# Regrouping the eight-wide heads of a decoder kernel: one 32-row score product per unit, one values block per step

## What is computed

```python
Q, K, V = split(x @ Wq), split(y @ Wk), split(y @ Wv)   # 16 heads of 8
scores = einsum('bhqd,bhkd->bhqk', Q, K) / sqrt(8)
attn = softmax(scores, axis=-1)
out = einsum('bhqk,bhkd->bhqd', attn, V).reshape(B, S, 128) @ Wo
```

## Time and profile before

| | us |
|---|---|
| median of 3 runs | 2144.5 (2141.21 to 2146.36) |
| span of the profiled execution | 2139.6 |
| PE busy in it | 1891.7 (88%) |
| DVE busy | 1520.1 (71%) |
| ACT busy | 1370.0 (64%) |
| POOL busy | 827.2 (39%) |

### The profile page before, as it was taken

How to read it: one execution, slowest core, us unless ns; L and a number is a source line. 1 busy time by engine, 2 the same in 40 slices (tenths; PEclk the granted TensorE clock), 3 DMA queues, 4 the chain that set the end, 5 groups by cost and what they waited for, 6 DMA issues and landing times. The chain is left out here.

```text
span 2139.6 us, 40133 instructions
## 1 busy us (share of the span) xinstructions
PE 1891.7 (88%) x13875; PEld 1361.0 (64%) x13945; DVE 1520.1 (71%) x4153; ACT 1370.0 (64%) x5428; POOL 827.2 (39%) x951
## 2 busy tenths in 40 slices
PE   6998989889998998998888999615899996899998
PEld 5757944535786965874444688404467775467776
DVE  4676788788655666779789855695876664786665
ACT  3686589827654587668963765343677774567666
POOL 2461056615432354025643533111543333543334
PEclk9999999979999999999998999867999998999999
DMA  5000000000001000000000000300000000000000
GB/s 228 1 1 1 2 1 1 1 1 2 1 2 34 1 2 1 1 2 1 1 1 1 1 2 1 111 0 13 1 2 1 1 1 24 1 1 1 1 1 11
DMA packets 6980, 24.79 MB, mean 12 GB/s; under 512 B 752, under 2 KB 3440, under 8 KB 6128
## 3 DMA queue, kind: packets, MB, share of 16 engines
q1 hardware_dynamic: 6768, 22.09, 2.8%
HBM read 21.04 MB, written 1.05 MB: 10 GB/s over the span
## 5 line engine op out<-in xcount | busy, mean ns | idle before, releaser
L1358 POOL TENSOR_TENSOR a_probs<-a_probs,a_rinv 128x512 f32<-128x512 f32 x352 | 367.3, 1044 | 421.9 <-DVE a_rinv L1191 417.5
L997 ACT ACTIVATE a_probs<-score_bank,a_negmax 128x128 f32<-128x128 f32 x896 | 315.7, 370 | 64.5 <-DVE a_negmax L1171 62.8
L1358 POOL TENSOR_TENSOR c_probs<-c_probs,c_rinv 128x512 f32<-128x512 f32 x192 | 201.1, 1047 | 296.2 <-DVE c_rinv L1191 294.2
L836 PEld LDWEIGHTS second_bank<-const,a_probs 128*128 128x128 f32 x1408 | 167.4, 142 | 193.4 <-DVE a_probs_t L1198 101.4
L803 PE MATMUL score_bank<-a_km,a_qg 128*128 128x512 f32 x512 | 267.6, 604 | 2.6 <-issue 0.9
L836 PE MATMUL second_bank<-const,a_probs 128*128 128x128 f32 x1408 | 218.4, 278 | 40.8 <-DVE a_probs_t L1198 32.8
L1366 POOL TENSOR_TENSOR a_rstd<-a_ve,neg_half 128x1 f32<-128x1 f32 x128 | 70.5, 551 | 357.6 <-DVE a_ve L1249 356.2
L1171 DVE TENSOR_REDUCE a_negmax<-score_bank 128x4 f32<-128x512 f32 x224 | 154.0, 687 | 67.7 <-PE score_bank L803 53.0
L997 ACT ACTIVATION_READ_ACCUMULATOR a_probs<-score_bank,a_negmax 128x1 f32 x896 | 188.2, 210 | 0.0
L1198 DVE COPY a_probs_t<-second_bank 128x512 f32<-128x512 f32 x272 | 179.6, 660 | 3.9 <-PE second_bank L836 3.9
L1021 ACT ACTIVATE c_probs_t<-second_bank 128x512 f32<-128x512 f32 x160 | 95.3, 595 | 109.9 <-PE second_bank L836 109.5
(11 more groups left out here) (308 smaller groups left out, 4590.3 us busy)
## 6 DMA issues: line engine op xcount, KB each, us to landing
w_L_ffn<-in_L_ffn SPq DMA_DIRECT2D x1, 3184.0 KB, 14.4
w_L_xattn<-in_L_xattn SPq DMA_DIRECT2D x1, 2112.0 KB, 24.2
w_L_xattn<-in_L_xattn SPq DMA_DIRECT2D x1, 2050.0 KB, 10.3
a_xt<-in_xT SPq DMA_DIRECT2D x3, 512.0 KB, 3.6
a_x<-in_x SPq DMA_DIRECT2D x3, 512.0 KB, 3.7
a_ct<-in_ctxT SPq DMA_DIRECT2D x3, 512.0 KB, 5.8
w_L_attn<-in_L_attn SPq DMA_DIRECT2D x1, 1345.5 KB, 17.2
w_L_attn<-in_L_attn SPq DMA_DIRECT2D x1, 1157.0 KB, 5.8
```

Of the source, the lines that this page charges most:

```text
L836: mm = pe.transpose(bank[:, j * S:(j + 1) * S], Pb[:, n % 4, j * S:(j + 1) * S], ident)
L997: op = act.activation(p, score_bank[n % 3][:, j * width:(j + 1) * width], ACT.Exp, bias=negmax[:, n % 4, j:j + 1], accum_out=rsum[:, n % 4 ...
L1358: pool.tensor_tensor(p, p, along(rinv[:, n % 4, 0:heads], 512 // heads), ALU.mult).then_inc(sems["norm_done"], 1)
```

## The change

Units are now cut the other way. Unit i takes the four heads 4i to 4i+3, which lie in rows 32i to 32i+31. Its score product uses these 32 rows alone: the queries' rows as they are, times `Kz`, the four copies of the keys that POOL spreads and scales by the eight rows of each e (it did that with the queries). The product still has 512 columns, and it is still one per unit and slot. `Km`, its four 32-row writes and `Qg` are gone: ACT writes the keys with one instruction, and the rotation on DVE is one instruction of 128x256 in place of five.

A value product for 32 partitions wants all of its heads' rows at once, so the values are now issued once per step, after i3, as 16 products, and `PT` keeps five units' transposes in place of two. `values` of i0, i1 and i2 issue nothing. The table of relative positions is read with a stride. `Q8` shares its storage with `K64` and `V64`, which are not live together.

```diff
+PT_RING = 5
...
+        if stage == "values":
+
+            return sum(self.kind(s) in SOFTMAX and (self.kind(s) not in H8 or i == 3) for s, i in self.units[:n + 1])
...
-            PT = sb(tag + "probs_t", [P, 2, 512], scope=scope)
+            PT = sb(tag + "probs_t", [P, PT_RING, 512], scope=scope)
...
-            Qg = sb(tag + "qg", [P, 2, 4, S], scope=scope)
-            Km = sb(tag + "km", [P, 2, 4, S], scope=scope)
+            Kz = sb(tag + "kz", [P, 2, 4, S], scope=scope)
...
-                            mm = pe.matmul(bank[:, :], Qg[:, plan.ring(s, 2), i, :], Km[:, plan.ring(s, 2), :, :].rearrange("p j k -> p (j k)"), start=mask != "causal", stop=True)
+                            rows = slice(32 * i, 32 * i + 32)
+                            mm = pe.matmul(bank[:, :], QK[rows, plan.ring(s, 2), 0, :], Kz[rows, plan.ring(s, 2), :, :].rearrange("p j k -> p (j k)"), start=mask != "causal", stop=True)
...
+                        if kind in H8:
+
+                            if i < 3:
+                                return
+                            for m in range(n - 3, n):
+                                wait_once(pe, sems[plan.copier(m)], plan.count(plan.copier(m), m))
...
-                            for j in range(4):
-                                mm = pe.matmul(value_bank[32 * j:32 * j + 32, 0:S], Vm[:, plan.ring(s, 2), i, 32 * j:32 * j + 32], pt[:, j * S:(j + 1) * S], start=i == 0, stop=i == 3)
+                            for e in range(4):
+                                for j in range(4):
+                                    mm = pe.matmul(value_bank[32 * j:32 * j + 32, 0:S], Vm[:, plan.ring(s, 2), e, 32 * j:32 * j + 32],
+                                                   PT[:, (n - 3 + j) % PT_RING, e * S:(e + 1) * S], start=e == 0, stop=e == 3)
...
-                            for j in range(4):
-                                rows = slice(32 * j, 32 * j + 32)
-                                op = act.activation(Km[rows, plan.ring(s, 2), j, :], bank[rows, S:2 * S], ACT.Identity, bias=W(s, "bk")[rows, :])
+                            op = act.activation(QK[:, plan.ring(s, 2), 1, :], bank[:, S:2 * S], ACT.Identity, bias=W(s, "bk"))
...
-                                dve.tensor_tensor(Km[rows, plan.ring(s, 2), j, :], QK[rows, plan.ring(s, 2), 1, :], RT2[rows, plan.ring(s, 2), 1, :], ALU.add)
-                            dve.tensor_tensor(QK[:, plan.ring(s, 2), 0, :], QK[:, plan.ring(s, 2), 0, :], RT2[:, plan.ring(s, 2), 0, :], ALU.add).then_inc(sems["rope_ready"], 1)
+                            dve.tensor_tensor(QK[:, plan.ring(s, 2), :, :], QK[:, plan.ring(s, 2), :, :], RT2[:, plan.ring(s, 2), :, :], ALU.add).then_inc(sems["rope_ready"], 1)
...
-                        pool.tensor_tensor(Qg[:, plan.ring(s, 2), :, :], over(QK[:, plan.ring(s, 2), 0, :], 4), along(head_scale, S), ALU.mult).then_inc(sems["masked"], 1)
+                        pool.tensor_tensor(Kz[:, plan.ring(s, 2), :, :], over(QK[:, plan.ring(s, 2), 1, :], 4), along(head_scale, S), ALU.mult).then_inc(sems["masked"], 1)
```

More of the change, by code:

```diff
@@ L542, in run_loop @@
             RT2 = sb(tag + "rt", [P, 2, 2, S], scope=scope)
-            Qg = sb(tag + "qg", [P, 2, 4, S], scope=scope)
-            Km = sb(tag + "km", [P, 2, 4, S], scope=scope)
+            Kz = sb(tag + "kz", [P, 2, 4, S], scope=scope)
             Vm = sb(tag + "vm", [P, 2, 4, D], scope=scope)
             nkeys = 2 * S if last_loop else S
-            V64 = sb(tag + "v64", [P, 2, nkeys // S, 1024], scope=scope)
             H = sb(tag + "h", [P, 4, 2, S], scope=scope)
@@ L550, in run_loop @@
             if last_loop:
+                V64 = sb(tag + "v64", [P, 2, nkeys // S, 1024], scope=scope)
                 Q64 = sb(tag + "q64", [P, 2, 16, S], scope=scope)
@@ L562, in run_loop @@
                 Qz = sb(tag + "qz", [P, 2, 8, 2, S], scope=scope)
-                K64 = sb(tag + "k64", [P, 2, 8, S], scope=scope)
+                ends = sb(tag + "ends", [P, 4096], scope=scope)
+                K64 = ends[:, 0:2048].rearrange("p (a c k) -> p a c k", a=2, c=8)
+                V64 = ends[:, 2048:4096].rearrange("p (a o d) -> p a o d", a=2, o=1)
                 CT = sb(tag + "ct", [P, G, S], scope=scope)
-                Q8 = sb(tag + "q8", [P, 3, 8, S], scope=scope)
+                Q8 = ends[:, 0:3072].rearrange("p (a h k) -> p a h k", a=3, h=8)
                 K8 = sb(tag + "k8", [P, 3, S], scope=scope)
@@ L591, in run_loop @@
             with nc.Block() as block:
-                @block.vector
-                def _(dve):
-                    dve.memset(Km[:, :, :, :], 0.0)
                 if not last_loop:
@@ L871, in values @@
                             wait_once(pe, sems["acc_done"], plan.count("acc", experts[-1]))
-                        pt = PT[:, n % 2, :]
+                        pt = PT[:, n % PT_RING, :]
                         if kind == "mqa":
@@ L1020, in turned @@
                             m = plan.count("second", n) - 1
-                            act.activation(PT[:, n % 2, :], second_of(n)[:, :], ACT.Copy).then_inc(sems["pt_act"], 1)
+                            act.activation(PT[:, n % PT_RING, :], second_of(n)[:, :], ACT.Copy).then_inc(sems["pt_act"], 1)
                     def outs(n):
@@ L1164, in front @@
                                 if kind == "h8p":
-                                    add = heads_view(W(s, "relpos")[:, i * 512:(i + 1) * 512], heads)
+                                    add = W(s, "relpos").rearrange("p (e u k) -> p u e k", e=4, u=4)[:, i, :, :]
                                 else:
@@ L1197, in back @@
                             dve.wait_ge(sems["second_ready"], m + 1)
-                            dve.tensor_copy(PT[:, n % 2, :], second_of(n)[:, :]).then_inc(sems["pt_dve"], 1)
+                            dve.tensor_copy(PT[:, n % PT_RING, :], second_of(n)[:, :]).then_inc(sems["pt_dve"], 1)
                         elif kind in STAGES["acc"]:
```

## The result

The changed kernel takes 2181.8 us (median of four, 2171.1 to 2192.4) against 2145.4 for the kernel before: a ratio of 1.0173, with a 95% interval of 1.0146 to 1.0200. The forecast was 2146 in a range of 2128 to 2166. The time lies above the range, on the side that had a chance of 0.39, and by a cause that had been given 0.04.

What follows compares the result with a forecast made beforehand. PE was taken as the main bound, busy 88% of the span. Stage terms summed to +0.8 us an iteration, +1.6 in both; 2139.6 + 1.6 + 4.9 = 2146 us, range 2128 to 2166.

Steps and rivals of the forecast that it cites:

- the clock: Rival: products on a quarter of the rows let the granted clock fall to half level, some +80 us; chance 0.04.
- What PE pays for the switch: Each unit's 32-row score product between 128-row products: 0.34 us, as 0.09 + 0.10 in, 0.09 out, 0.05 for transposes' weights.
- The 0.44: Upper bound per unit if the second pass's weights also load in the open; sum some 25 us higher; not adopted.
- The rival of a free switch: Rival: the 32-row product switches freely, so 1.36 us a step go, about -85, giving 2060 us; chance 0.04.
- The values block: Values once per step on PE: 0.81 us from first to last start, 1.20 with the switches.
- `L1_attn`: Stage term: step from 10.32 to 10.17 us, wait for ACT replaced by a wait for scores; -1.2 us an iteration.
- `L1_xattn`: Stage term: four steps waiting for the turned sequence gain 0.8 us each, other idle time shrinks; -4.3 us an iteration.
- The causal stages: Stage terms with the mask product: +4.6 us each on PE, less absorbed idle: `L0_xattn` +2.8, `L2_attn` +2.3, `L3_attn` +1.2.
- a clock below 1.00 in a stage: Sign that would show the forecast wrong: the granted clock falls below 1.00 in some stage.
- The sum without the clock: Whole kernel: stage terms of +0.8 us an iteration, +1.6 in both, giving 2146 us at unchanged clock.
- the likeliest case: Forecast case: sum within about 8 us of 2146, own range 2138 to 2155; chance 0.47.
- The first rival: Rival: ACT falls behind in slots 2 and 3, PE pays 34 of +40 us; half is about 2162; chance 0.27.

## Why the prediction was wrong, point by point

**The step that failed** is the clock. The sum held it at 1.00 and so gave it a term of zero; as a rival it had 0.04 and +80 us, with the words "No row shows such a fall behind a row-tiled product, and none excludes it". The runs show that editing the height of the product alone moves the clock (0.852, 0.928, 0.955 and 0.956 with 8, 32, 64 and 128 rows), that 32 rows are enough to lower it in the kernel before (0.866), and that it costs the change about 45 us. The size of the rival was of the right order; its chance was not. An effect that no row excludes had been priced as if a row did. The range, too, should have reached to it, since the change makes 320 such products where the trace of before had no 512-column one at all.

**What PE pays for the switch**, 0.34 us a unit, was right (1.51 to 1.85), and so were its parts: 0.08 and 0.10 in, 0.09 out and 0.06 for the transposes' weights, forecast as 0.09, 0.10, 0.09 and 0.05. Of 320 x 0.34 = 109 us, 58 reach the end; most of the rest fills idle time in `L1_attn`, `L1_xattn` and `L3_attn`. The 0.44 that follows from the rule on weight loads in the Trainium skill, "TensorE: Matmul & The Clock Gate", Part 3, was not seen. Both passes' weights are loaded by 133.97, while the first pass, on the same rows, runs on to the start of the second at 134.21:

```profile
133.68 0.29 PEld L805 LDWEIGHTS score_bank<-a_kz,a_qk 32*128 32x128 f32 x2 [0.32 <-issue]
```

The rival of a free switch is out as well: 2060 was its time, and 2078 is what the kernel does when the switches really go.

**The values block** was right too: 0.81 + 0.20 was forecast from its first start to the next product's, 1.01 is measured, and L731 behind it holds PE 0.33 where its two passes are 0.22, the 0.10 of weights in the open.

**`L1_attn`** was forecast at 10.17 us a step, with ACT's wait gone and DVE waiting for scores. DVE's timeline of after, one step apart, against the earlier trace rows:

```profile
332.92 0.69 DVE L1174 TENSOR_TENSOR a_probs<-score_bank,w_L_attn 128x512 f32<-128x512 f32 x1 [0.58 <-PE score_bank L805]
...
343.07 0.69 DVE L1174 TENSOR_TENSOR a_probs<-score_bank,w_L_attn 128x512 f32<-128x512 f32 x1 [0.58 <-PE score_bank L805]
```

That is 10.15, with a wait of 0.58 for the scores. The stage is 6.1 longer all the same, because of one step of 13.9 and one of 12.65 in it. The second is no part of the 45 us: with 64 rows it takes 12.65 as well (10.69 before), and the stage is only 0.2 shorter than before, where 1.2 was forecast.

**`L1_xattn`** was to become 4.3 shorter, with the wait for the turn gone. PE's only wait there is now the one below, in place of the earlier trace rows; steps went from 9.88 to 9.22 and from 8.94 to 8.76. With the clock kept (64 rows) the stretch is 69.7, that is 5.1 shorter. In the changed kernel one step of 13.4 takes it back.

```profile
PE second_bank L838 <- DVE a_probs_t L1203: 0.6, 1, 0.6
```

**The causal stages.** `L0_xattn` was forecast at +2.8 and is +2.2. `L2_attn` (+2.3) is +0.2: more of its idle time was absorbed than the half I took. `L3_attn` (+1.2) is 0.0 and -1.5 with 64 rows and +6.0 and +12.5 in the changed kernel; its first three steps take 13.2, 18.2 and 18.8 in the second iteration where they took 7.4, 10.5 and 17.8. I had named "a clock below 1.00 in a stage" and "`L3_attn` longer by 4" as what would prove me wrong, and both came.

**The sum without the clock** was nearly right: 2146 us forecast and 2136.5 in the 64-row kernel, within the range though below the likeliest case's own 2138. It is lower mainly because `L2_attn` and `L3_attn` came out some 2 us an iteration below their terms, while `L1_attn` came out 1.0 above; so part of the agreement is errors that cancel. The first rival, that the relief does not reach PE, is not seen: PE's waits for the transposes' copies are 7.0 us in `L1_attn`, where they were 8.7, and 0.8, 0.6 and nothing in the other stages of loop A.

**What stays open.** The runs do not tell how much full-height work, or how placed, keeps the clock, nor why the added product left some slow steps in `L1_attn` of the changed kernel when it left none there in the kernel before with 32-row scores. Nor do they tell whether an added product of few rows would have done the same.

## What to carry to other kernels

Before cutting a product to fewer rows, count what PE will see: not only the time of a switch (here 0.34 us a unit), but a clock that may halve for whole steps, and price a cost that no row excludes by a test, not by a small chance. In a kernel near PE's bound the relief of the other engines was worth more (-45 us) than the bunched values it came with (-17), and taking work off PE alone was worth nothing until ACT and DVE had room. When work is handed to a lightly used engine, give it its own slot: two operations in a row cost 20 us more than the same two apart.

## What the runs showed of the hardware

In these kernels TensorE's granted clock depended on how many rows a product used, not only on whether PE was busy. With the score products at 8, 32, 64 and 128 rows it was 0.852, 0.928, 0.955 and 0.956, while PE was busy 92, 90, 90 and 88% of the span. The Trainium skill, "TensorE: Matmul & The Clock Gate", Part 1, says that the gate is set by how busy the PE has been recently; by busy time alone the first kernel would have the highest clock of the four, so here the measurement says more than the page.

Between 64 and 32 rows the issue times are equal (L799 to L805 0.31, L805 to the transposes 1.05), so these two heights pay the same switch; only the clock tells them apart. At the lower level the two passes of 512 columns, with the first weights and the way out, take 2.00 us instead of 1.05. One bf16 product of 128 rows and 512 columns ahead of each low one, 0.22 us at full clock (130.84 to 131.06 above), took a step of `L1_attn` from 17.05 to 10.44, though it did not hold the clock in every stage.
